# Handing R and H of a recurrent kernel on in two pieces of two channel groups

## The reference

```python
def step(H, xs):
    xz, xr, xh = xs
    Z = jax.nn.sigmoid(xz + H @ Whz.T + bhz)
    R = jax.nn.sigmoid(xr + H @ Whr.T + bhr)
    H_tilda = jnp.tanh(xh + R * H @ Whh.T + bhh)
    H_new = Z * H + (1.0 - Z) * H_tilda
    Y = H_new @ Whq.T + bhq
    return (H_new, Y)
_, Ys = jax.lax.scan(step, h0, (Xz, Xr, Xh))
...
x = x + transpose(Ys)
```

## Time and profile before

| | us |
|---|---|
| median of 3 runs | 2157.72 (2157.51 to 2157.75) |
| the profiled execution's own time | 2158.46 |
| its span, first to last instruction | 2156.7 |
| PE busy | 2142.5 (99%) |
| PEld busy | 2127.9 (99%) |
| DVE busy | 1622.0 (75%) |
| ACT busy | 845.4 (39%) |
| POOL busy | 167.0 (8%) |

### The profile page before, as it was taken

How to read it: one execution, slowest core, us unless ns; L and a number is a source line. 1 busy time by engine, 2 the same in 40 slices (tenths; PEclk the granted TensorE clock), 3 DMA queues, 4 the chain that set the end, 5 groups by cost and what they waited for, 6 DMA issues and landing times.

```text
span 2156.7 us, 187383 instructions
## 1 busy us (share of the span) xinstructions
PE 2142.5 (99%) x82136; PEld 2127.9 (99%) x82136; DVE 1622.0 (75%) x9469; ACT 845.4 (39%) x4864; POOL 167.0 (8%) x520
## 2 busy tenths in 40 slices
PE   8999999999999999999999999999999999999999
PEld 7999999999999999999999999999999999999998
DVE  5777777777777777777777777777777777777777
ACT  2333433344334333433343334333343334333433
POOL 1000000000000000000000000000000000000000
PEclk9999999999999999999999999999999999999999
DMA  4000000000000000000000010001000100010000
GB/s 160 27 28 25 24 26 27 25 24 25 27 26 24 24 27 27 24 24 27 28 24 24 26 29 24 24 26 29 24 24 26 29 24 24 26 29 24 24 26 27
DMA packets 111764, 62.66 MB, mean 29 GB/s; under 512 B 28801, under 2 KB 110849, under 8 KB 110977
## 3 DMA queue, kind: packets, MB, share of 16 engines
q1 hardware_dynamic: 111744, 62.37, 9.9%
HBM read 45.55 MB, written 16.78 MB: 29 GB/s over the span
## 4 chain that ended last, share of the span: by engine, by line
PE 99%; DMA 1%; DVE 0%; issue 0%; ACT 0%; SPq 0%; DVEq 0%
PE gates L396 60%; PE p_bank L321 16%; PE gates L321 12%; PE y_bank L329 10%; DMA bias_in<-in_b_gate 0%; DMA out<-y_io 0%; DMA y_io<-in_x_res 0%; DVE t L746 0%; DVE t L732 0%; DVE scanned L689 0%; DVE pre_t L625 0%; PE p_bank L428 0%; DVE yt L680 0%; ACT scan_on L611 0%; ACT gates L617 0%
## 5 line engine op out<-in xcount | busy, mean ns | idle before, releaser
L396 PE MATMUL gates<-wh,scanned 128*16 128x128 f32 x32768 | 1048.6, 273 | 4.0 <-DVE scanned L689 2.3
L396 PEld LDWEIGHTS gates<-wh,scanned 128*16 128x16 f32 x32768 | 944.9, 104 | 8.6 <-DVE scanned L689 3.4
L625 DVE STREAM_TRANSPOSE pre_t<-gates 128x32 f32<-128x32 f32 (+2 forms) x3584 | 618.1, 216 | 194.0 <-PE gates L396 142.1
L396 PE MATMUL gates<-wh,reset_state 128*16 128x128 f32 (+1 forms) x16384 | 600.8, 273 | 1.5 <-issue 1.2
L396 PEld LDWEIGHTS gates<-wh,reset_state 128*16 128x16 f32 (+1 forms) x16384 | 471.3, 103 | 4.7 <-issue 2.0
L596 ACT ACTIVATE r_gate<-pre_t 128x16 f32<-128x16 f32 (+1 forms) x1536 | 234.7, 215 | 496.9 <-DVE pre_t L625 496.9
L321 PE MATMUL p_bank<-t,s 128*32 128x192 f32 x6096 | 361.8, 326 | 0.1
L611 ACT ACTIVATE scan_on<-pre_t 128x16 f32<-128x16 f32 (+1 forms) x1536 | 238.3, 219 | 266.6 <-DVE pre_t L625 266.6
L689 DVE TENSOR_TENSOR_SCAN scanned<-scan_by,scan_on 128x32 f32<-128x32 f32 x2048 | 301.0, 209 | 28.6
L321 PEld LDWEIGHTS p_bank<-t,s 128*32 128x32 f32 x6096 | 245.3, 110 | 2.7 <-issue 0.5
L743 DVE TENSOR_TENSOR scan_on<-z_gate,scanned 128x64 f32<-128x64 f32 x512 | 116.6, 228 | 174.1 <-ACT z_gate L600 174.1
(11 more groups left out here) (76 smaller groups left out, 1599.5 us busy)
## 6 DMA issues: line engine op xcount, KB each, us to landing
xr<-in_x_t SPq DMA_DIRECT2D x128, 128.0 KB, 2.1
y_io<-in_x_res SPq DMA_DIRECT2D x256, 64.0 KB, 1.9
out<-y_io SPq DMA_DIRECT2D x256, 64.0 KB, 1.6
x_b<-in_x_t SPq DMA_DIRECT2D x127, 32.0 KB, 1.7
wx_v<-in_w_xv SPq DMA_DIRECT2D x1, 1536.0 KB, 6.8
wx_u<-in_w_xu SPq DMA_DIRECT2D x1, 1536.0 KB, 11.8
wh<-in_w_hr SPq DMA_DIRECT2D x1, 1024.0 KB, 12.9
wh<-in_w_hz SPq DMA_DIRECT2D x1, 1024.0 KB, 14.9
```

Source lines behind the costliest of these rows:

```text
L396: mm = nc.tensor.matmul(gate_rows(g, par, slice(Q * j, Q * j + rows)), of, w, start=False, stop=(m == G - 1), skip_group_check=True)
L625: nc.vector.transpose(flat(pre_t[g][:, a:b]), gate_part(g, par, a, b)).then_inc(done, 1)
```

## The change

One line. `PARTS` has two pieces of two groups each in place of three pieces (one, one, two groups). Everything that is built from `PARTS` and its length `N` follows: two transposes, two activations and two multiplies for R, two transposes and two activations for H, two semaphores in place of three for each stage of the two hand-ons, and two waits on PE in place of three, at groups 0 and 2. The scans remain one for each group, and `state_ready[0]` is raised after the second of them.

```diff
-PARTS = [(0, 1), (1, 2), (2, 4)]
+PARTS = [(0, 2), (2, 4)]
 N = len(PARTS)
```

## The result

| | before | after |
|---|---|---|
| median, us (22 runs each) | 2157.36 | 2160.86 |
| ratio after to before, 95% interval | | 1.0017 [1.0011, 1.0023] |
| profiled execution, us | 2158.46 | 2161.35 |
| its span, us | 2156.7 | 2159.6 |

The change costs 3.5 us. The forecast was 43 us. The sign was right and the size wrong by a factor of twelve; at 0.17% the loss lies just inside the 0.2% that I had called "same" and given 0.03, and its interval reaches a little past it. The runs of each kernel differ among themselves by up to 2.7 us.

A forecast was written before the change was run, and what follows sets the result against it. PE's full stream was taken to bound the kernel. R's 0.22 and the state's 0.11 gave 0.33 a turn, 41.6 us over 126 turns, plus 1.5 for the ends: 43 us, 2201, range 2188 to 2215.

The forecast's parts named there:

- The step that failed: At R's hand-on at c = 0: H's first matmul, at 1008.36, was taken as the due time of PE's stream.
- R's terms: Lateness at R's four hand-ons: 0.045 at c = 0 and 2, 0.06 at c = 1, 0.07 at c = 3; 0.22 a turn.
- The state's term after c = 0: State's hand-on after c = 0: load and matmul ready at 1010.54 against 1010.43 due, 0.11 late a turn.
- Next to no room here: At R's hand-on at c = 0: the semaphore already releases the load, which comes only 0.03 ahead of its matmul.
- The later start of the transposes: Named sign of being wrong: R's transposes start later than now, relative to the last product of R.
- Rival 3: Whole loop: no change, PE hides a late load fully and catches up after the wait; 2157 to 2159, chance 0.03.
- Rivals 1 and 2: Cost a turn: 1, larger, 0.45, 2216, chance 0.05; 2, smaller, 0.095, 2171, chance 0.05.
- Rival 4: Waits on PE: faster, eight fewer a turn at 0.005 each save 0.04 a turn, 5 us, 2153; chance 0.01.
- rival 2's lower price: Smaller loss with only one of its two savings, leads or widths: 0.19 to 0.235 a turn, 2182 to 2189.
- missing leads: At the five late hand-ons: if the released load needs no time, leads are 0.095 less in sum.

The follow-up runs named there:

- R alone: Kernel before with only R's hand-on in two pieces of two groups, the state's still in three: 2157.87 us against 2157.05, ratio 1.0003.
- reversed strips: Kernel before with the four column strips issued in reverse order everywhere on PE: 2156.84 us against 2157.20, ratio 1.0000.
- instructions put back: Changed kernel with its second piece cut in two (pieces of two, one and one groups): 2161.02 us, ratio 1.0018 to the kernel before.
- second and third experiment: Second: kernel before with only the state's hand-on in two pieces, 2161.9 us. Third: changed kernel with its second piece cut in two, 2161.02 us.
- the dose: Kernel before with larger first pieces: R in three and one groups 2172.61 us, in one piece 2207.22; state likewise 2196.28 and 2275.55.

## Why the prediction was wrong, point by point

- **What bounds the kernel.** Right: PE's stream. The turn is 16.613 in three kernels (before, R alone, reversed strips), and in no run does a saving on DVE or ACT get below it.
- **How late the first pieces come.** Right to 0.01: transpose to load 0.795 and 0.943 forecast, 0.79 and 0.94 measured; wider transpose 0.25, sigmoid 0.228 to 0.230, multiply 0.19, tanh 0.235, second scan 0.11.
- **The step that failed** is "Its matmul starts at 1008.36, where the stream of PE is due to go on". It took the first strip for the stream. Every "due" in the sum (1008.36, 1012.40, 1004.20, 1010.43, 1014.59, 1002.24) was that of a strip with a lead of 0.11 to 0.14. With the due time of the fourth strip, all four of R's terms (0.22) vanish. The state's term after c = 0 (0.11) shrinks: the strip sets out from a transpose that is 0.03 later and is due 0.14 later, 0.11 + 0.03 - 0.14 + the 0.02 between first and fourth strip is about 0.02; the traces give 0.026.
- **"Next to no room here"** drew on the load being released by the semaphore already. That was a true observation (0.05 behind the multiply in both places), and the conclusion false: the three strips run as far ahead as the release lets them. With R alone in two pieces, H's first load comes 0.06 later (1.100 against 1.038 after R's last product) and the lead is 0.066 smaller. A load that is just in time for its own strip says nothing of the strip that is last.
- **The later start of the transposes**, 0.340 in place of 0.311 after R's last product, I hadn't foreseen; I had named it as a thing that would make me wrong, and it worked against the kernel, not for it. It is 0.339 to 0.343 in every kernel whose strips are in phase (0.376 at c = 0 with R in one piece), and 0.310 or 0.311 in all others.
- **Rival 3** (no change) came nearest. I had met it with "a matmul that starts late has no idle slot to recover in", true for a strip, but three of the four didn't need to recover. It isn't the mechanism that I had given it either, since PE doesn't catch up after a stall: in the changed kernel the strips stay in phase for the rest of the turn. The rule that I had set beside it (the Trainium skill, TensorE: Matmul & The Clock Gate, Step-by-step: what each phase is for: loads are pulled ahead of matmuls under way) agrees with the rows as far as loads go: the load at 1008.33 starts ahead of the read-out's matmul at 1008.38. It is not what hid the lateness. The same section of the Trainium skill has matmuls stay in program order; across the strips the recorded starts here don't (H at 1008.36, the read-out issued ahead of it at 1008.38).
- **The other rivals.** Rivals 1 and 2 kept the same wrong due time; the range, built from them, could not hold the result. Rival 4's saving doesn't show: putting eight waits a turn back leaves the turn at 16.639 (instructions put back), and taking four away leaves it at 16.613 (R alone).
- **The sums.** They add up but for the last us: rival 2's lower price comes to 2183, not 2182, and 0.43 and 0.45 a turn with the ends to 2213 and 2216, not 2212 and 2215. The lower bound of 0.23 a turn is the whole price of the missing leads, not half-way to it. None of this brings the result into the range.
- **What the removed work brings**: nothing, as forecast; the second and third experiment show it from both sides.

Settled by the runs: the loss is the state's hand-on after c = 0, at 0.026 a turn. Left open: how the lead arises. In the kernel before it is 0.18 to 0.20 in R and Z of the very first step; at c = 1 to 3 of the first turn, where PE waits for hand-ons, the four strips end within 0.02 of each other, and from the second turn on the lead is back. The changed kernel has it in its second and third turn too and loses it there; it doesn't come back in the rest of the loop, where each turn has one load that all four strips wait for.

No version here beats the kernel before. Its turn is PE's own work already, so the most that fewer pieces could give is the same time with less to do on DVE and ACT: R in two pieces and the state in three does that.

## What to carry to other kernels

When products run on several strips of the array, read the due time from the strip that is last, and look at all matmuls under way around a hand-on, not at the first that depends on it. A load that waits for its semaphore in a full stream isn't yet at the edge; the dose that first lengthens the loop shows where the edge is, and here the next 0.065 of R then cost 0.07 at each of the four hand-ons (17.013 against 16.727 a turn). That holds for this kernel; no other was run. A fall of PEld's busy share at an equal number of loads, here from 99% to 94%, can be the sign that such a lead has been used up.

## What the runs showed of the hardware

- Matmuls of different strips don't all start in the order of the program: three strips of H start at 1008.36, the fourth strip's read-out, issued ahead of them, at 1008.38 and 1008.44.
- The transposes that wait for a product start 0.311 after its last matmul's start while the strips are staggered, 0.34 when they are in phase.
- In the first and last turn of the kernel before, a load released while PE stands idle costs 0.01 with 16 columns and 0.025 with 32: the first matmul then lasts 0.28 or 0.30 and the next of its strip follows 0.12 or 0.135 later, not 0.109.
